# Delta stage: 32x32 blocks turned on VectorE and placed by transfers, in place of transposes on TensorE

## The chip, the core and the metric

The kernel runs on one core of one Trainium2 chip. The metric is the device time of one execution in microseconds (us). The core has TensorE (PE in the profile, with PEld for its weight loads), VectorE (DVE), ScalarE (ACT), GpSimd (POOL), and SyncE (SP), which here issues nearly all transfers (DMAs), in order.

## What is computed

A row of 1024 tokens of width 256 passes four blocks with residual additions: an attention block, a first mixture of experts, a gated delta rule layer, and a second mixture of experts. The change lies in the gated delta rule layer (`_L1_attn_ref`), 32 value heads on 16 key heads, chunks of 64 tokens, cut here to its core:

```python
qkv = silu(causal_conv1d(qkv, conv_weight))            # per channel, 4 taps
q, k = l2norm(q) * Dk ** (-0.5), l2norm(k)
attn = -(k_beta @ k.T * decay_mask), strictly lower    # per chunk
attn = (I - attn)^-1                                   # row by row in the reference
value_corrected = attn @ v_beta
k_cumdecay = attn @ (k_beta * exp(g))
for c in chunks:                                       # carries the state
    v_prime = value_corrected - k_cumdecay @ state
    out = q @ state * exp(g) + (q @ k.T * decay) @ v_prime
    state = state * exp(g_last) + (k * kd).T @ v_prime
core = rmsnorm(out * silu(z), norm_weight)
x = x + core @ W_out
```

## The kernel before

All work of the layer is in `delta1_phase`. It takes the key heads one after another; what belongs to one key head (one key, one query, GR = 2 value heads) is called a round here, g = 0 to 15. Tokens lie in TT = 8 tiles of 128. The code handles the state in steps t = 0 to 7 of 128 tokens.

Of one round, these are the steps, under the names in the order tables. On TensorE `proj j c` projects key, query and two values (j = 0 to 3) with channels on the partitions, `products i` multiplies keys by keys and queries, and `kturn`, `qturn`, `vturn h` transpose eight 128x128 tiles each, so that tokens lie on the partitions. `l0p, l0y, l0x, l1p, l1y, l2p, l2y` build the inverse of a 128x128 matrix out of its solved 16x16 diagonal blocks, in many small matmuls. `gates i` project z. `ks, qs, y, kv, iv` with a step number carry the state: ks and y make the corrected values, kv the new state, qs and iv the output. `out_turn b` transposes eight tiles of the normalised output and `out_mm b i` multiplies them by W_out, for halves b = 0, 1. VectorE has the convolution taps (`tap`, line 1647), the scaling of keys, values and outputs (`kb`, `vturn` 1711, `yn` 1786), the product with the decay (`products` 1702), the residual `r` 1757, the state 1766, the sum `gather` 1779 and the addition to x (1792). ScalarE has the first tap and silu, the decay's exp, the squares for the norms (`ksq`, `qsq`, `sq2`), and copies out of PSUM (`kturn` 1823, `ys` 1911, `out_turn` 1926). GpSimd solves the 16x16 blocks (`solve`), scales keys (`kout` 1952), applies the gate (`gate` 1988) and the norm's power (`norm`).

SyncE moves, per round, the 16x16 blocks out to DRAM and back in another layout (`blocks`, lines 1355 and 1359), the solved blocks out and back (`solved`, 1377 to 1384), decay rows (`rows`), weights of the round after next (`weights` 1320) and a slice of W_out (`wo` 1348). So the inverse of a round hangs on this chain: products of VectorE (semaphore `ai_s`), `blocks`, `solve`, `solved`, `l0p`.

The order of the work is written out by hand, one table for each engine (`PE_ORDER`, `DVE_ORDER`, `ACT_ORDER`, `POOL_ORDER`, `SP_ORDER`), run once for each round. In the table `this` stands for the round's own state part, `next` for the projections and products of the round after it, and `prev` for what is left of the round before. `loop` writes the steps in that order, so each engine has a fixed sequence, and its waits are on semaphores.

## Time and profile before

| | us |
|---|---|
| median of 3 runs | 2077.16 (2075.91 to 2077.48) |
| the profiled execution, its own time | 2069.65 |
| its span on the core | 2067.9 |
| first matmul of the delta layer to the last addition to x | 622.00 to 1844.3 |
| start of l0p in round 1, 14 and 15 | 764.54, 1704.47, 1774.98 |
| PE, DVE, ACT, POOL busy over the span | 1650.5, 1178.3, 894.6, 569.4 |

The page gives busy time of each engine and its costliest lines. It lists a median time to landing only for some transfers. The timeline gives instructions in order of time, merged where they follow each other: start, duration, engine, line, operation, output from input, count, and in brackets the idle time before it with what ended it. "issue" is idle time in which the engine waited for nothing that the profile shows. Matmuls are pipelined, so the distance from one start to the next says more than a duration. A matmul in 32 bits is two records; a transpose is one.

### The profile page before, as it was taken

What the parts mean: (1) busy time and instruction counts of PE and PEld (TensorE: products, weight loads), DVE (VectorE), ACT (ScalarE), POOL (GpSimd) and SP (SyncE); (2) the same over time, 40 slices, a digit from 0 to 9 for tenths busy, and PEclk for the clock granted to TensorE, in tenths of its full rate; (3) what the DMA queues carried; (4) which work ended last, traced back from release to release, by engine and by line L of the source; (5) the groups of instructions that cost most, each with busy time, mean ns of one, the idle gap of its engine ahead of it and who ended that gap; (6) DMA issues with size and microseconds to landing.
All of it is one profiled execution on the core that took longest, in us unless ns stands there. A gap on an engine that the chain in (4) does not pass through costs nothing. (4 is left out here: it accounts for less than half of the span.)

```text
span 2067.9 us, 43100 instructions
## 1 busy us (share of the span) xinstructions
PE 1650.5 (80%) x16669; PEld 1199.2 (58%) x16669; DVE 1178.3 (57%) x2439; ACT 894.6 (43%) x2414; POOL 569.4 (28%) x958
## 2 busy tenths in 40 slices
PE   5878952566025899999999999999999999857998
PEld 2443341455012677777777767777777777744555
DVE  6774149111545467667667666776676677333444
ACT  2225920112014464655665566566556556321111
...
GB/s 208 1 2 2 1 70 1 124 155 130 166 20 50 39 46 27 26 51 35 22 48 51 27 26 52 38 37 30 51 33 23 50 35 12 16 1 31 38 38 43
DMA packets 175331, 95.95 MB, mean 46 GB/s; under 512 B 98467, under 2 KB 165923, under 8 KB 175136
## 3 DMA queue, kind: packets, MB, share of 16 engines
...
## 5 line engine op out<-in xcount | busy, mean ns | idle before, releaser
L1647 DVE SCALAR_TENSOR_TENSOR d_conv<-d_big,d_cw,d_conv 128x1023 f32<-128x1023 f32 (+2 forms) x192 | 245.3, 1278 | 42.9 <-ACT d_conv L1808 40.0
L1406 PE MATMUL d_big<-all_xn_t,d_w 128*128 128x512 f32 x512 | 248.3, 614 | 26.4 <-DMA d_w<-in_L_attn_W_qkvz 15.5
L1988 POOL TENSOR_TENSOR d_y<-d_y,all_xn 128x256 f32<-128x256 f32 x128 | 96.5, 754 | 259.3 <-DVE d_y L1779 217.8
L1406 PEld LDWEIGHTS d_big<-all_xn_t,d_w 128*128 128x128 f32 x512 | 95.7, 197 | 105.9 <-issue 90.5
L1619 PE MATMUL d_big<-d_wo,d_yt 128*128 128x256 f32 x512 | 145.7, 442 | 3.7 <-issue 2.8
L1944 POOL TENSOR_TENSOR d_sv<-d_ek,d_half 128x8 f32<-128x8 f32 x16 | 26.2, 1637 | 425.7 <-DVE d_ek L1673 396.3
L2150 PE MATMUL e_gu<-all_xn_t,e_up_w 128*128 128x512 f32 x272 | 121.9, 602 | 15.4 <-DMA e_dn_w<-in_L_ffn_Wd 15.4
L1808 ACT ACTIVATE d_conv<-d_big,d_cw 128x1024 f32<-128x1024 f32 x64 | 71.4, 1116 | 134.0 <-issue 78.3
L1619 PEld LDWEIGHTS d_big<-d_wo,d_yt 128*128 128x128 f32 x512 | 111.8, 227 | 22.9 <-issue 4.1
L1911 ACT COPY d_ys<-d_big 128x128 f32<-128x128 f32 x256 | 60.4, 268 | 142.9 <-PE d_big L1575 123.8
L1549 PE MATMUL d_big<-d_w,all_xn_t 128*128 128x256 f32 x512 | 118.3, 379 | 1.5 <-DVE d_vs L1711 1.5
L1549 PEld LDWEIGHTS d_big<-d_w,all_xn_t 128*128 128x128 f32 x512 | 96.0, 190 | 27.1 <-issue 14.4
L1702 DVE SCALAR_TENSOR_TENSOR d_AI<-d_big,d_b_col,d_decay 128x256 f32<-128x256 f32 x256 | 105.8, 476 | 6.6 <-PE d_big L1436 6.6
L323 DVE TENSOR_REDUCE a_neg_max<-a_big 128x1 f32<-128x128 f32 (+7 forms) x128 | 90.0, 752 | 32.7 <-PE a_big L256 32.6
L1918 ACT ACTIVATE d_junk<-d_y 128x128 f32<-128x128 f32 x256 | 79.8, 312 | 47.3 <-POOL d_y L1988 43.0
L2150 PEld LDWEIGHTS e_gu<-all_xn_t,e_up_w 128*128 128x128 f32 x272 | 52.5, 193 | 74.6 <-issue 73.8
L147 PE MATMUL ln_turned<-all_ident,all_xn 128*128 128x128 f32 x64 | 17.5, 443 | 91.0 <-DVE all_xn L127 91.0
L473 ACT ACTIVATE a_probs<-a_big 128x512 f32<-128x512 f32 (+3 forms) x192 | 77.0, 513 | 20.6 <-PE a_big L406 18.5
L1973 POOL TENSOR_TENSOR d_blk_ty<-d_blk_ty,d_blk_p 128x15 f32<-128x15 f32 (+7 forms) x240 | 80.2, 334 | 18.8
L2183 DVE TENSOR_TENSOR e_h<-e_act_g,e_gu 128x512 f32<-128x512 f32 x34 | 23.4, 687 | 107.3 <-ACT e_act_g L2171 107.3
L1786 DVE TENSOR_TENSOR d_y<-d_y,d_rn 128x1024 f32<-128x1024 f32 x32 | 43.4, 1357 | 68.0 <-POOL d_rn L2004 68.0
L2171 ACT ACTIVATE e_act_g<-e_gu 128x512 f32<-128x512 f32 x34 | 20.3, 597 | 142.4 <-PE e_gu L2150 142.4
...
## 6 DMA issues: line engine op xcount, KB each, us to landing
...
c_rows<-ranked_scratch SPq DMA_DIRECT2D x4, 1024.0 KB
c_rows<-ranked_scratch ACTq DMA_DIRECT2D x4, 1024.0 KB
...
```

The source lines that it names most:

```text
L323: dve.tensor_reduce(neg_max[:, h, q:q + 1], big[2 + q % 2][:, :, :].rearrange("p c n -> p (c n)")[:, 0:(q + 1) * P], AX.X, ALU.max, negate ...
L473: act.activation(probs[:, n % NPB, off:512], bank[n % NST][:, off:512], ACT.Exp).then_inc(exp_done, 1)
L1406: mm = pe.matmul(big[0][:, c, :], w_sb[par][:, k, n * DK:(n + 1) * DK], xn_t[:, k, c * 512:(c + 1) * 512], start=(k == 0), stop=(k == KD - 1))
L1549: mm = pe.matmul(bank[6 + i % 2][:, (t % 2) * 256:(t % 2) * 256 + 256], xn_t[:, k, t * P:(t + 1) * P], w_sb[par][:, k, 4 * DK:6 * DK], sta ...
L1619: mm = pe.matmul(bank[6 + i][:, r * 256:r * 256 + 256], yt[:, h, 2 * i + r, :], wo_sb[:, h, :], start=(h == 0), stop=(h == GR - 1), skip_g ...
L1647: dve.scalar_tensor_tensor(conv[:, sh:T], src[:, 0:T - sh], cw[:, bass.ds(g, 1), COLUMN_OF[j], 3 - sh], conv[:, sh:T], ALU.mult, ALU.add). ...
L1702: ins = dve.scalar_tensor_tensor(AI[par][:, h * TT + t, :, :], bank[6 + i % 2][:, (t % 2) * 256:(t % 2) * 256 + 256].rearrange("p (a i) -> ...
L1808: act.activation(conv[:, :], big[0][:, :, :].rearrange("p c n -> p (c n)"), ACT.Copy, scale=cw[:, bass.ds(g, 1), COLUMN_OF[j], 3]).then_in ...
L1918: act.activation(junk[:, :], y[:, t, h, :], ACT.Square, accum_out=ss2[:, i:i + 1]).then_inc(s["sq2_s"], 1)
L1973: pool.tensor_tensor(T_[:, j + 1:BL, 0:j + 1], T_[:, j + 1:BL, 0:j + 1], blk_p[:, 0:rows, 0:j + 1], ALU.subtract).then_inc(s["sol_v"], 1)
L1988: pool.tensor_tensor(part, part, zs[:, t, :], ALU.mult).then_inc(s["yg_s"], 1)
L2150: mm = pe.matmul(gu_ps[c][:, n, :], up_w[par][:, n, k, :], xn_t[:, k, c * 512:(c + 1) * 512], start=(k == 0), stop=(k == KD - 1))
```

## The change

- `kturn`, `qturn`, `vturn`, `out_turn` leave TensorE and ScalarE. In their place VectorE turns each 32x32 block within its own 32 partitions (`kq_turn a`, `v_turn h`, `y_turn b`, all STREAM_TRANSPOSE of 128x1024), and SyncE places the blocks by way of DRAM: `kq_out a`, `kq_in a`, `v_out`, `v_in`, `y_out b`, `y_in b`.
- The values are scaled in place by GpSimd (`vs`), which also takes over `yn` and `cross` from VectorE. norm_weight is multiplied into W_out once a round (`wo` on GpSimd).
- The squares of q are taken from SBUF. `products 0` waits for silu and the gates' buffers only.
- All five order tables are new. `out_mm 0` moves from its own round into the next, `proj 2` and `proj 3` stand elsewhere, and steps 2 to 5 of the state follow each other with little between.

```diff
 SP_ORDER
-    this rows, solved, weights; next blocks; prev wo
+    this solved, v_in; next kq_out 0, kq_in 0; prev y_out 0; next kq_out 1; this weights; next kq_in 1, rows; prev y_in
+    0, y_out 1; next blocks; prev y_in 1, wo; next v_out
...
+            def kq_out(g, par, a):
+                sp.wait_ge(s["kq_x"], g * 2 + a + 1)
...
+                sp.dma_start(kq_dram[a].rearrange("q r b n -> (q r) b n"),
+                             turned[:, :, a * TT:(a + 1) * TT, :].rearrange("p b t r -> p b (t r)")).then_inc(s[f"kq_out{a}"], 16)
+            def kq_in(g, par, a):
...
+                    if a == 0:
+                        sp.wait_ge(s["kout_s"], g * 2)
...
+                sp.wait_ge(s[f"kq_out{a}"], g * 16 + 16)
+                for b in range(NQ):
+                    sp.dma_start(kq_tok[QB * b:QB * b + QB, :, a * TT:(a + 1) * TT, :].rearrange("p q t r -> p q (t r)"),
+                                 kq_dram[a, :, :, b, :].rearrange("q r n -> r q n")).then_inc(s[f"kq_in{a}"], 16)
+            def v_out(g, par):
+                sp.wait_ge(s["v_x"], g * 2 + 2)
...
+                sp.dma_start(v_dram.rearrange("q r b n -> (q r) (b n)"), turned[:, :, :, :].rearrange("p b a r -> p (b a r)")
+                             ).then_inc(s["v_out"], 16)
+            def y_in(g, par, b):
...
+                sp.wait_ge(s["y_out"], g * 128 + 64 * b + 64)
+                for q in range(NQ):
+                    sp.dma_start(yt[:, :, QB * q:QB * q + QB], y_dram[q].rearrange("e r (a n) -> (e r) a n", n=QB)
+                                 ).then_inc(s["yt_in"], 16)
...
 on TensorE
-            def kturn(g, par):
-            def qturn(g, par):
-            def vturn(g, par, h):
-            def out_turn(g, par, b):
...
 on VectorE
-            def vturn(g, par, h):
-            def yn(g, par, b):
+            def v_turn(g, par, h):
+                dve.wait_ge(s["silu_s"], g * NJ + h + 3)
...
+                dve.transpose(turned[:, :, h * TT:(h + 1) * TT, :], vt[:, :].rearrange("p (t q r) -> p q t r", q=NQ, r=QB)
+                              ).then_inc(s["v_x"], 1)
...
 on ScalarE
-            def kturn(g, par):
-            def out_turn(g, par, b):
...
 on GpSimd
+            def vs_(g, par, h):
...
+                pool.tensor_tensor(mine, mine, sv[:, :].unsqueeze(1).unsqueeze(3).broadcast_to([P, NQ, TT, QB]), ALU.mult
+                                   ).then_inc(s["vs_s"], 1)
+            def yn(g, par, b):
```

TensorE around l0p of one round. Before (in the names, d_X and d_Y are the solved blocks, all_ident marks a transpose, d_w the projections and gates, d_wo out_mm):

```order
L1549 MATMUL d_big<-d_w,all_xn_t 128x256 x4
L1406 MATMUL d_big<-all_xn_t,d_w 128x512 x2
L1463 MATMUL d_big<-d_X,d_AI 32x16 x64
L1610 MATMUL d_big<-all_ident,d_y 128x128 x8
L1474 MATMUL d_big<-d_Y,d_P 32x32 x64
L1486 MATMUL d_big<-d_P,d_Y 32x32 x48
L1619 MATMUL d_big<-d_wo,d_yt 128x256 x8
L1499 MATMUL d_big<-d_Xc,d_AI 32x32 x32
L1414 MATMUL d_big<-all_ident,d_kq 128x128 x8
L1406 MATMUL d_big<-all_xn_t,d_w 128x512 x2
```

And with the change:

```order
L1610 MATMUL d_big<-d_S,d_kq 128x256
L1623 MATMUL d_big<-d_rv,d_Y 128x128 x2
L1475 MATMUL d_big<-all_xn_t,d_w 128x512 x4
L1505 MATMUL d_big<-d_X,d_AI 32x16 x64
L1641 MATMUL d_big<-d_ys,d_AI 128x128 x2
L1516 MATMUL d_big<-d_Y,d_P 32x32 x64
L1528 MATMUL d_big<-d_P,d_Y 32x32 x48
L1475 MATMUL d_big<-all_xn_t,d_w 128x512 x4
L1541 MATMUL d_big<-d_Xc,d_AI 32x32 x32
L1594 MATMUL d_big<-d_w,all_xn_t 128x256 x4
```

The transposes between l0p and l0y and behind l1p are gone. Behind l0x stands the projection of the next round's j = 2 where out_mm stood, and behind l1p a gates step.

SyncE between the blocks of one round and the solved blocks that l0p needs. Before:

```order
L1355 DMA blocks_scratch<-d_AI 16x16x16 x8
L1359 DMA d_blk_at<-blocks_scratch 128x256
L1348 DMA d_wo<-in_L_attn_W_out 128x2x256
L1328 DMA d_G<-decay_rows_scratch 64x4x256
```

And with the change, in that place and up to the first load of solved blocks:

```order
L1363 DMA blocks_scratch<-d_AI 16x16x16 x8
L1367 DMA d_blk_at<-blocks_scratch 128x256
L1453 DMA d_yt<-turned_y_scratch 128x8x32 x4
L1356 DMA d_wo<-in_L_attn_W_out 128x2x256
L1423 DMA turned_v_scratch<-d_turned 128x2048
L1385 DMA solved_scratch<-d_blk_ty 128x512
L1391 DMA d_X<-solved_scratch 16x16x16
```

The decay rows are gone from ahead of the solved blocks (they stand earlier now), and the 1024 KB of turned values go out directly ahead of them.

## Rows read from the trace of the kernel before

**Rows 1.** Windows: stretch, length, busy PE, PEld, DVE, ACT, POOL, granted clock, DMA share, GB/s.
```profile
772.00:776.00 4.00, 3.40 (x85) 3.07 (x86) 1.60 (x3) 3.07 (x4) 0.00 (x0) 0.50 0.02 4
...
1260.00:1330.00 70.00, 67.31 (x880) 53.29 (x879) 50.43 (x92) 43.30 (x124) 29.21 (x56) 1.00 0.18 39
```

**Rows 2.** Timeline of TensorE, the start of l0p in rounds 0, 1, 8, 9, 15.
```profile
693.79 1.91 PE L1463 MATMUL d_big<-d_X,d_AI 32*32 32x16 f32 x128 [4.79 <-DMA d_Y<-solved_scratch]
...
764.54 1.26 PE L1463 MATMUL d_big<-d_X,d_AI 32*32 32x16 f32 x128
...
1275.62 1.25 PE L1463 MATMUL d_big<-d_X,d_AI 32*32 32x16 f32 x128
...
1343.89 1.26 PE L1463 MATMUL d_big<-d_X,d_AI 32*32 32x16 f32 x128
...
1774.98 1.90 PE L1463 MATMUL d_big<-d_X,d_AI 32*32 32x16 f32 x128 [2.84 <-DMA d_Y<-solved_scratch]
```

**Rows 3.** Timeline of TensorE, a set of eight transposes and the step behind it.
```profile
1218.08 1.09 PE L1414 MATMUL d_big<-all_ident,d_kq 128*128 128x128 f32 x8
1219.01 1.88 PE L1406 MATMUL d_big<-all_xn_t,d_w 128*128 128x512 f32 x4
```

**Rows 4.** Timeline of TensorE, idle in the small matmuls of rounds 5 and 15.
```profile
1063.56 0.71 PE L1474 MATMUL d_big<-d_Y,d_P 32*32 32x32 f32 x59 [1.18 <-issue]
...
1066.91 0.50 PE L1486 MATMUL d_big<-d_P,d_Y 32*32 32x32 f32 x27 [1.88 <-issue]
...
1783.20 0.25 PE L1486 MATMUL d_big<-d_P,d_Y 32*32 32x32 f32 x4 [1.19 <-issue]
```

**Rows 5.** Timeline of TensorE, steps of the state: ks 5, then kv 5.
```profile
1249.07 0.68 PE L1558 MATMUL d_big<-d_S,d_kq 128*128 128x128 f32 x4
...
1251.05 0.71 PE L1584 MATMUL d_big<-d_ys,d_kout 128*128 128x128 f32 x4 [0.24 <-ACT d_ys L1911]
```

**Rows 6.** Timeline of TensorE ahead of l0p of round 8: vturn 1 and gates 3.
```profile
1258.94 1.06 PE L1414 MATMUL d_big<-all_ident,d_vt 128*128 128x128 f32 x8
...
1271.95 1.89 PE L1549 MATMUL d_big<-d_w,all_xn_t 128*128 128x256 f32 x8
```

**Rows 7.** Groups by line: busy us, mean ns of one, then idle before and what ended it.
```profile
L1647 DVE SCALAR_TENSOR_TENSOR d_conv<-d_big,d_cw,d_conv 128x1023 f32<-128x1023 f32 (+2 forms) x192 | 245.3, 1278 | 42.9 <-ACT d_conv L1808 40.0
...
L1786 DVE TENSOR_TENSOR d_y<-d_y,d_rn 128x1024 f32<-128x1024 f32 x32 | 43.4, 1357 | 68.0 <-POOL d_rn L2004 68.0
...
L1952 POOL TENSOR_TENSOR d_kout<-d_k_tok,d_kxb 128x1024 f32<-128x1024 f32 x32 | 61.5, 1921 | 2.6 <-POOL d_blk_ty L1978 0.2
...
L1711 DVE TENSOR_TENSOR d_vs<-d_big,d_sv 128x1024 f32<-128x1024 f32 x32 | 38.9, 1216 | 4.6 <-PE d_big L1414 4.5
...
L1816 ACT ACTIVATE d_vt<-d_conv 128x1024 f32<-128x1024 f32 x32 | 33.9, 1061 | 5.7 <-DVE d_conv L1647 5.2
```

**Rows 8.** Timeline of SyncE's queue: first load of round 0, then blocks and solved of round 8.
```profile
686.49 0.33 SPq L1383 DMA_DIRECT2D d_X<-solved_scratch  x1
...
1243.52 3.74 SPq L1355 DMA_DIRECT2D blocks_scratch<-d_AI  x8
...
1265.19 0.33 SPq L1377 DMA_DIRECT2D solved_scratch<-d_blk_ty  x1
1267.22 0.33 SPq L1383 DMA_DIRECT2D d_X<-solved_scratch  x1
```

**Rows 9.** Two transfers of 1024 KB: DMA issues (us to landing), timeline of SyncE's queue.
```profile
tokens_scratch<-all_xn SPq DMA_DIRECT2D x1, 1024.0 KB, 5.9
...
2062.68 0.38 SPq L2204 DMA_DIRECT2D out<-all_x  x1
```

**Rows 10.** Windows, while the solved blocks (3072 pieces of 64 bytes) are loaded.
```profile
1267.20:1275.60 8.40, 8.36 (x33) 5.59 (x32) 4.01 (x4) 5.26 (x19) 6.88 (x7) 1.00 0.31 32
```

**Rows 11.** Timeline of the last round: VectorE's yn 1, then TensorE's out_mm.
```profile
1832.88 1.22 DVE L1786 TENSOR_TENSOR d_y<-d_y,d_rn 128x1024 f32<-128x1024 f32 x1 [4.16 <-POOL d_rn L2004]
...
1837.00 6.57 PE L1619 MATMUL d_big<-d_wo,d_yt 128*128 128x256 f32 x16 [0.87 <-ACT d_yt L1926]
```

More of the change, by code:

```diff
@@ new lines @@
+    0, proj 1 1; this l0p; prev iv 7; this l0y, l0x; next proj 2 0, proj 2 1; this l1p, gates 3, l1y; next products 0;
+    this l2p 0, l2p 1; next proj 3 0; this l2y 0; next products 1; this l2y 1; next products 2; this y 0; next products
+    3; this kv 0; next proj 3 1; this ks 1, iv 0, qs 1, y 1; prev out_mm 0 0; this kv 1, iv 1, ks 2; prev out_mm 0 1;
+    this y 2, qs 2, kv 2, iv 2, ks 3, qs 3, y 3, kv 3, iv 3, ks 4, qs 4, y 4, kv 4, iv 4, ks 5, qs 5, y 5, kv 5, iv 5;
+    prev out_mm 1 0; this ks 6; prev out_mm 1 1; this y 6, qs 6, kv 6
@@ L1188 @@
 """)
 DVE_ORDER = steps_of("""
-    prev state 6, r 7, gather 6; this vturn 1; next shift 0, tap 0 1, tap 0 2, tap 0 3, shift 1; prev gather 7, yn 1;
-    this l0p; next tap 1 1, tap 1 2; this qe; next tap 1 3; this l0x; prev out_mm 1 0, out_mm 1 1; next cross; this l1p,
-    l1y, l2p; next tap 2 1; this l2y; next tap 2 2, kb; this state 0, gather 0, r 1; next tap 2 3, products 0; this
-    state 1; next products 1; this r 2; next products 2; this state 2, gather 1, r 3; next products 3; this gather 2,
@@ L1195 @@
-    gather 3, state 3, r 4; next vturn 0; this state 4, gather 4, r 5, yn 0, state 5; next tap 3 1; this r 6; next tap 3
-    2, tap 3 3; this gather 5, out_mm 0 0, out_mm 0 1
+    next shift 0, tap 0 1, tap 0 2; prev r 7; next tap 0 3; prev gather 6; next shift 1; this qe; next kq_turn 0; prev
+    y_turn 0; next tap 1 1; this l0p; next tap 1 2; prev gather 7; next tap 1 3; this l0x; next kq_turn 1; this l1p;
+    next tap 2 1, tap 2 2; this l1y; next tap 2 3; this l2p; next kb, products 0; this l2y; next products 1, products 2;
@@ L1197 @@
+    this state 0; prev y_turn 1; this r 1; next products 3; this gather 0, state 1, gather 1, r 2; prev out_mm 0 0; next
+    tap 3 1; this state 2, r 3, gather 2, state 3, r 4, gather 3, state 4, r 5, gather 4; prev out_mm 0 1; this state 5;
+    next v_turn 0, tap 3 2; this r 6; next tap 3 3; this gather 5; prev out_mm 1 0; this state 6; next v_turn 1; prev
+    out_mm 1 1
 """)
 ACT_ORDER = steps_of("""
-    next tap0 0; prev o1 7; this gates 0, gates 1; prev ys 7, sq2 5, sq2 6, sq2 7; this gates 2; next silu 0; this gates
@@ L1201 @@
[L1201 to L1204 removed]
+    prev sq2 2; next tap0 0; prev o1 6; this gates 0; prev sq2 3; this gates 1; prev sq2 4; next silu 0; prev o1 7, ys
@@ L1205 @@
+    7; next tap0 1; prev sq2 5; next decay; this gates 2, l0y; next silu 1; prev sq2 6; next tap0 2; this l1p; next ksq
+    0, ksq 1, ksq 2, ksq 3; this l1y, gates 3, l2p; prev sq2 7; this l2y, ys 0; next qsq 0; this o1 1, ys 1; next silu
+    2, tap0 3; this ys 2, o1 2, ys 3, o1 3, ys 4, o1 4, ys 5, sq2 0, o1 5; next qsq 1; this ys 6; next silu 3; this sq2
+    1
 """)
 POOL_ORDER = steps_of("""
-    this solve 2, solve 3, solve 4; prev gate 5; this kout; prev gate 6, gate 7, norm 1; next kb; this gate 0, gate 1,
@@ L1391, in _ @@
             sp.wait_ge(s["const_s"], 12)
-            loop(sp, SP_ORDER, dict(blocks=blocks, solved=solved, weights=weights_after, rows=rows_after, wo=wo_after))
+            loop(sp, SP_ORDER, dict(kq_out=kq_out, kq_in=kq_in, v_out=v_out, v_in=v_in, y_out=y_out, y_in=y_in, blocks=blocks, solved=solved, weights=weights_after, rows=rows_after, wo=wo_after))
         @block.tensor
```

247 lines of the change are left out of this document (140 added, 107 removed).

## The prediction

> **What bounds the kernel now.** First the windows over the delta stage, in stretches of 70 us: TensorE is busy 65 to 67 us of 70, VectorE 50, ScalarE 43, GpSimd 29, and the transfer engines 18% [rows 1]. So a round costs what TensorE's list costs, plus what TensorE waits. Second the timeline of TensorE by round, at the start of l0p: from round 1 to 15 it is (1774.98 - 764.54) / 14 = 72.2 us a round, and the leanest, round 8, takes 1343.89 - 1275.62 = 68.3 us [rows 2]. Third, what the 3.9 us between the two are: inside l0y and l0x TensorE stops twice with no releaser ("issue"), 1.18 and 1.88 us in round 5 [rows 4], and behind such a pair, in round 1, the granted clock is 0.50 from 772 to 776, its lower level of 1.2 GHz, where it is 1.00 through the lean round [rows 1]. Fourth, SyncE's queue: from the end of products (`ai_s`, 1243.52) to l0p (1275.62) 32.1 us pass [rows 2, 8], and l0p starts directly as the last solved blocks land. So the chain of the inverse has no slack today; TensorE's list and that chain are in balance.
>
> **What leaves TensorE.** Eight transposes take 1219.01 - 1218.08 = 0.93 us [rows 3]; a round has six such sets (kturn, qturn, two vturn, two out_turn): 6 x 0.93 = 5.6 us. All lies on the path, since TensorE is the bound: 72.2 - 5.6 = 66.6. The Trainium skill (VectorE: DVE Perf Modes, Rules for kernel authors) speaks against the change: transpose 128x128 on TensorE if PSUM will do. By that rule, as I read it, the saving would be nothing or less. The row shows what it is worth here, 0.12 us for a tile on the engine that is the bound.
>
> **What VectorE gets.** It loses two vturn of 1.22 us, two yn of 1.36 [rows 7] and cross (about 1.2, the same length of row): 6.4 us. It gets six STREAM_TRANSPOSE of 128x1024. The trace has none. The nearest row is the scaling of the same 1024 elements, 1.22 us; the other end is twice that, 2.4, and nothing suggests less than 1.2. I take 1.25, so 7.5 us against 6.4, and VectorE stays at some 48 of 68 us. At 2.4 it would be 55, still no bound, but one of the six lies on a path, below.
>
> **GpSimd** gets two scalings of values, two yn, cross and the W_out product. By kout, 1.92 us for 1024 elements [rows 7], that is 5 x 1.92 + 1 = 10.6 us: 29 becomes some 40 of 68. Not the bound. ScalarE loses one copy and four halves of a copy, 3 to 4 us.
>
> **State steps in a row.** Steps 2 to 5 have no filler now. From ks 5 to kv 5 is 1.98 us for three steps that need 1.35 [rows 5], and the same again at kv to ks; such a step costs about 0.7 us more than its matmuls. Before, the two steps that stood alone and the short waits round y 0, y 1 and step 2 summed to about 3 us; with the new table I count 2.6. I put this at nothing. Two small waits are new: l2p has only products 0 (0.9 us) ahead of it to cover VectorE's copy, which stands behind a tap of 1.28 us [rows 7]: 0.6 us. And VectorE has tap 1 1 ahead of l0p's result, which costs up to 1.1 us in a round where TensorE does not wait at l0p, and nothing where it does.
>
> **The wait that the change adds.** SyncE sends v_out (1024 KB) directly ahead of `solved`, whose result l0p needs. v_out waits for v_turn 1, which waits for silu 3, behind ys 6 on ScalarE. Both sides start at kv 6. On TensorE, the steps between kv 6 and l0p are those of before without vturn and with iv 6 and gates 3 changed: 1275.62 - 1258.94 = 16.7, less 0.9, less gates 3 at 1.8 [rows 2, 6] = 14.0 us. On the other side: from the end of kv 6 silu 3 and v_turn 1 end 2.0 us later (1.06 + 1.25, begun just before kv 6 starts [rows 7]); v_out lands 5.9 us after its issue by the other store of 1024 KB, or at most 5.2 by the last store of the kernel, issued at 2062.68 in a span that ends at 2067.9 [rows 9]; the 256 KB of `solved` alone take 2.0 us (1265.19 to 1267.22), of which I let 1.0 stand behind v_out (0 to 2.0); from there to l0p it is 7.3 us in round 0 (686.49 to 693.79) and 8.4 in round 8 [rows 2, 8]. Sum 15.5 to 17.3, or 1.5 to 3.3 us more than TensorE's 14.0; I take 2.4. Queued behind v_out on SyncE are `solved`, v_in and kq_out 0, kq_in 0; who waits is l0p, and TensorE idles.
>
> A wait before l0p gives something back: in round 15, which waits 2.84 us there [rows 2], only one issue gap of 1.19 us follows instead of two of 3.1 in sum [rows 4]. I take 1.0 us. So a round is 66.6 + 0.6 + 2.4 - 1.0 = 68.6; without that wait it would be 66.6 + 0.6 + 1.1 = 68.3. The two agree, which makes 68.5 likely: 72.2 - 68.5 = 3.7 us saved, over 15 rounds 56 us.
>
> **Other transfers.** I count from the start of l0p, by the list of steps; an issue on SyncE takes 3.74 / 8 = 0.47 us [rows 8]. k: v_in's four issues end at about 0.5, kq_out 0 is behind them and lands, with v_in's 1024 KB ahead of it, at 5 to 6. kout on GpSimd, which kq_in 0 waits for too, ends at about 4, eight steps behind solve. Then four issues and a landing of 2 us: 9 to 10. Squares on ScalarE for 3.5 us make 13, and products 0 on VectorE has to be done by 20, when products 2 wants its buffer on TensorE, so the landing is needed by some 13. y: y_in 0 is issued behind the weights (which wait for gates 3, at 12), kq_in 1 and the decay rows, at 17 to 19, and lands at 23; out_mm 0 0 comes at 27. y_in 1 is issued behind blocks, at 34, and lands at 40; out_mm 1 0 comes at 42, behind iv 5. The blocks leave at 28 instead of 36 after l0p, which gives the chain of the inverse (32.1 us from there) its slack: 28 + 32 = 60, were it not for v_out. All hidden, with 2 to 4 us of cover; if one is gone, TensorE stops by what is missing, once a round. Bytes: 6 MB a round more on a queue that is busy 18% [rows 1].
>
> **Prologue and epilogue.** The prologue gains and loses about the same: k and q take 4 to 6 us longer to reach their squares, but products no longer waits for the squares of q. The epilogue is exposed. Before, from the end of yn (1832.88 + 1.22) to out_mm (1837.00) 2.9 us pass [rows 11]. Now each half takes y_turn 1.25, four issues of 0.47 and a landing of 2 for y_out, the same four issues and some 5.4 for y_in: 12.4 us. The two halves overlap in part, but y_in 1 waits until out_mm 0 has read its tile. I get 12 us more at the end (7 to 20).
>
> **Sum.** Against the profiled execution's 2069.65: - 56 + 12 = - 44, 2026. The three runs have a median of 2077.16, 7.5 above that execution; the same difference against it is 2033.
>
> **Rivals.**
> A, the forecast: a round of 67.5 to 69.7 us, 2018 to 2051. For it: two ways of counting meet there.
> B, the tables fit closer than I count, nothing new waits: 66.6 us, 15 x 5.6 = 84 less, 12 more: 2005. For it: v_out's data may go in parallel with `solved`, and tap 1 1 may be early enough. Against it: both go down one queue, in order.
> C, slower: the same place, l0p behind v_out. If block transposes take 2.4 us (1.2 more), v_out 5.9, `solved` its full 2.0 behind it and the loads 8.4, the wait is 2.0 + 1.2 + 5.9 + 2.0 + 8.4 - 14.0 = 5.5 us, and if nothing is given back at the issue gaps, a round takes 66.6 + 0.6 + 5.5 = 72.7. That is 8 us more in 15 rounds, and the epilogue: 2097. It decides from a round of 71.4, a wait of 4.2 us. For it: TensorE lost its clock behind the 2.84 us of round 15, where l0p took 1.90 us instead of 1.26 [rows 2]. Against: it takes all high ends.
> D, slower: the pieces of 128 bytes of y_in (4096 for each half). In the loads of solved blocks 31% of 16 engines over 8.4 us moved 3072 pieces of 64 bytes [rows 10], 14 ns a piece. At that price a half takes 3.6 us. The other end is the store in pieces of 1 KB, 5.9 us for 1024 of them [rows 9], 92 ns with all latency in it. From about 39 ns on, y_in 1 makes out_mm 1 0 and ks 6 wait 3 us a round; at 45 ns both halves wait, some 8 us in sum, and 15 x (68.5 + 8 - 72.2) + 12 gives 2154. The Trainium skill (DMA: Bandwidth & Descriptors, Specifications) asks for 512 bytes or more for line rate; it would make such pieces dear. The solved blocks show that pieces of 64 bytes are not.
> The change does what it says, by the order of instructions; that it would not is no case.
>
> **How the numbers follow.** A 0.42, B 0.17, C 0.20, D 0.07, and 0.14 for a round between 69.7 and 71.8 (some cover gone once), which is 2051 to 2083 and holds most of "same". Time: that of A. Range: from B's 2000 up to 2098, which takes C in and leaves D out. Within 0.2% (4 us, about what this kernel's measurement can tell) I put 0.06; faster 0.42 + 0.17 + 0.08 = 0.67; slower 0.27.
>
> **What would show it.** TensorE's transposes gone and l0p to l0p at 68 to 69 us in the middle rounds. Before l0p an idle time of 1.5 to 3.3 us that ends with a DMA of the solved blocks: right for A. If none, B. If over 4, C. The landing of v_out and of `solved` in the list of DMA issues. STREAM_TRANSPOSE at 1.2 or 2.4 us. out_mm waiting on d_yt by a DMA says D. products on VectorE waiting for kb would say that the k path was longer than I placed it. The stretch from yn 1 of the last round to the last addition to x, 12 us longer. I would be wrong most easily if a wait that I call covered, by 2 to 4 us, is not.

## The result, and the profile after

The changed kernel takes 2056.5 us (median of 4 runs, 2055.2 to 2060.0), the kernel before 2076.5 on the same chip (2073.2 to 2077.5). The ratio is 0.9908, 95% interval 0.9891 to 0.9925. On a second chip it was 0.9933 (0.9911 to 0.9954). So it is faster, by 20 us where 44 were forecast. The profiled execution took 2057.01 us with a span of 2055.3, which is 12.6 less than the profiled execution before.

The timeline of TensorE at the start of l0p (L1505 now) in rounds 1, 8, 14 and 15. In brackets is the idle time before the row, with what ended it.

```profile
763.54 1.25 PE L1505 MATMUL d_big<-d_X,d_AI 32*32 32x16 f32 x128 [1.30 <-DMA d_Y<-solved_scratch]
...
1255.84 1.26 PE L1505 MATMUL d_big<-d_X,d_AI 32*32 32x16 f32 x128
...
1672.86 1.26 PE L1505 MATMUL d_big<-d_X,d_AI 32*32 32x16 f32 x128
...
1742.65 1.90 PE L1505 MATMUL d_big<-d_X,d_AI 32*32 32x16 f32 x128 [6.85 <-DMA d_Y<-solved_scratch]
```

A round is (1672.86 - 763.54) / 13 = 69.95 us, where it was (1704.47 - 764.54) / 13 = 72.30. That is 2.35 saved, not 3.7. The windows over these 13 rounds, before and after (the columns are those of [rows 1]):

```profile
764.54:1704.47 939.93, 880.98 (x11312) 698.93 (x11311) 639.10 (x1144) 563.21 (x1612) 345.95 (x638) 0.97 0.17 37
```

```profile
763.54:1672.86 909.32, 822.10 (x10687) 632.62 (x10687) 684.60 (x1157) 522.57 (x1546) 486.60 (x718) 0.93 0.56 129
```

TensorE is busy 58.9 us less, 4.5 a round instead of the 5.6 of six sets of transposes, since its granted clock fell from 0.97 to 0.93. It is idle 909.32 - 822.10 = 87.2 us instead of 59.0, 2.2 a round more. 72.3 - 4.5 + 2.2 is the 69.95. The waits of TensorE in that stretch say where (us in total, times, longest). First before, then after:

```profile
PE d_big L1486 <- issue: 19.5, 10, 2.2
PE d_big L1474 <- issue: 17.6, 12, 1.8
```

```profile
PE d_big L1516 <- issue: 44.8, 13, 5.2
PE d_big L1516 <- DVE d_P L1770: 10.0, 10, 1.3
PE d_big L1528 <- issue: 9.1, 6, 1.8
PE d_big L1505 <- DMA d_Y<-solved_scratch: 7.6, 8, 2.2
PE d_big L1661 <- DMA d_yt<-turned_y_scratch: 5.5, 5, 1.5
PE d_big L1641 <- issue: 5.5, 1, 5.5
```

L1474 and L1486 were l0y and l0x, now L1516 and L1528. L1641 is iv 7, which now stands between l0p and l0y. Idle time there that no semaphore explains grew from 37.1 to 59.4 us, from 2.9 to 4.6 a round. This is the larger part of what is missing.

**What "issue" is here.** The timeline of TensorE in round 7:

```profile
1187.45 1.25 PE L1505 MATMUL d_big<-d_X,d_AI 32*32 32x16 f32 x128 [0.95 <-DMA d_Y<-solved_scratch]
1188.70 0.68 PE L1641 MATMUL d_big<-d_ys,d_AI 128*128 128x128 f32 x4
1189.66 1.13 PE L1516 MATMUL d_big<-d_Y,d_P 32*32 32x32 f32 x111 [0.27 <-DVE d_P L1770]
1194.68 0.47 PE L1516 MATMUL d_big<-d_Y,d_P 32*32 32x32 f32 x17 [3.89 <-issue]
1194.92 1.90 PE L1528 MATMUL d_big<-d_P,d_Y 32*32 32x32 f32 x96
1196.75 4.86 PE L1475 MATMUL d_big<-all_xn_t,d_w 128*128 128x512 f32 x8
```

TensorE stops in the middle of l0y, at 1190.8. The list of DMA queues has a queue of kind "instruction". In the quarter of a microsecond from 1191.75 it begins one packet of 0.02 MB (packets, MB, share of 16 engines):

```profile
q1 hardware_dynamic: 39, 0.05, 98.0%
q8 instruction: 1, 0.02, 33.0%
```

That share of 0.25 us is 1.32 us of one engine. The packet starts at about 1192.0, and the gap ends at 1194.68. Before, ahead of the 1.18 us gap of round 5 [rows 4], the same view of the quarter from 1061.00:

```profile
q1 hardware_dynamic: 23, 0.04, 44.4%
q8 instruction: 1, 0.02, 23.3%
```

That packet took 0.93 us and began at about 1061.2, 1.2 us before TensorE ran dry at 1062.38. The later one began 1.2 us after TensorE ran dry. From l0p of round 1 to l0p of round 14 the kernel before has 23 idle times of 1 us or more on TensorE, and all 23 end 1.1 to 1.7 us behind the end of such a packet. Their packet starts on average 0.65 us before the idle time does. After the change 30 idle times are that long. 11 of them end with a semaphore. The 19 marked issue all end 1.2 to 1.6 us behind the end of a packet, which starts on average 0.53 us after the idle time does.

What is late is the start of the packet and not its length: over these 13 rounds a packet takes 1.08 us in the mean before and 1.13 after. But the first one behind the start of l0p begins 2.1 us after it before, and 4.8 us after it with the change.

So what is missing are TensorE's instructions, which come by DMA. In this run of small matmuls they are used up faster than they come. The Trainium skill (Runtime: NRT & Kernel Launch, Instruction fetch mechanics) says that an engine's sequencer fetches its instructions in blocks of 16 KiB by a DMA queue of its own. The packets of 0.02 MB agree. It calls the cost mostly hidden, and here the trace doesn't agree: 59.4 us of idle in 13 rounds. What filled the engines meanwhile is seen in the windows of the same stretch:

```profile
1189.00:1192.00 3.00, 1.51 (x115) 1.24 (x113) 3.00 (x5) 2.94 (x4) 2.17 (x2) 1.00 1.09 242
1192.00:1195.00 3.00, 0.32 (x23) 0.32 (x26) 0.23 (x1) 1.73 (x2) 1.49 (x1) 0.55 0.55 178
```

The DMA share is 1.09 at 242 GB/s: v_in and kq_out 0, issued at 1186.1 and 1188.2. In the kernel before, the same place of round 5 reads:

```profile
1061.00:1064.00 3.00, 1.82 (x127) 1.56 (x127) 2.96 (x4) 2.94 (x4) 0.00 (x0) 1.00 0.07 25
```

There the share is 0.07. From 1.5 to 4.5 us after the start of l0p the share is 0.23 in the mean of the 13 rounds before, and 1.05 after. What in the engines holds the packet back these views don't show; that the bulk transfers do it is tried below. After the change the granted clock also falls from 1.00 to the lower level of 1.2 GHz while TensorE waits, and the projection behind it (L1475) runs slow, 4.86 us for eight matmuls that take 3.60 at the full clock (1252.31 to 1255.84).

The order of SyncE around l0p of round 8:

```profile
1209.22 9.47 SPq L1453 DMA_DIRECT2D d_yt<-turned_y_scratch  x4
...
1243.83 0.34 SPq L1423 DMA_DIRECT2D turned_v_scratch<-d_turned  x1
1244.37 0.32 SPq L1385 DMA_DIRECT2D solved_scratch<-d_blk_ty  x1
1248.39 0.32 SPq L1391 DMA_DIRECT2D d_X<-solved_scratch  x1
```

Groups by line, the new operations of VectorE and GpSimd (busy us, mean ns of one, idle before):

```profile
L1756 DVE STREAM_TRANSPOSE d_turned<-d_vt 128x1024 f32<-128x1024 f32 x32 | 39.7, 1242 | 1.5 <-ACT d_vt L1870 1.4
L2066 POOL TENSOR_TENSOR d_y<-d_y,d_rn 128x1024 f32<-128x1024 f32 x32 | 60.7, 1897 | 2.5
```

### The profile page after: what moved, and what is told of

It reads as the page before. It is cut to its first block and busy times, and to the rows that moved or that the text cites. A ratio compares the mean times of both kernels' runs of the same rounds, so it can differ in the third digit from the quotient of the medians.

```text
span 2055.3 us, 42263 instructions
## 1 busy us (share of the span) xinstructions
PE 1579.2 (77%) x15901; PEld 1117.7 (54%) x15901; DVE 1225.2 (60%) x2456; ACT 845.9 (41%) x2334; POOL 742.0 (36%) x1053
## 5 line engine op out<-in xcount | busy, mean ns | idle before, releaser
L1475 PE MATMUL d_big<-all_xn_t,d_w 128*128 128x512 f32 x512 | 274.1, 675 | 37.5 <-DVE d_conv L1690 22.0
L2044 POOL TENSOR_TENSOR d_y<-d_y,all_xn 128x256 f32<-128x256 f32 x128 | 115.7, 904 | 230.9 <-DVE d_y L1837 123.7
L1475 PEld LDWEIGHTS d_big<-all_xn_t,d_w 128*128 128x128 f32 x512 | 103.4, 218 | 141.6 <-issue 121.1
L1661 PE MATMUL d_big<-d_wo,d_yt 128*128 128x256 f32 x512 | 126.2, 392 | 24.4 <-DMA d_yt<-turned_y_scratch 23.6
L1661 PEld LDWEIGHTS d_big<-d_wo,d_yt 128*128 128x128 f32 x512 | 95.7, 197 | 37.3 <-issue 19.2
L1822 DVE SCALAR_TENSOR_TENSOR d_S<-d_S,l_gamma,d_big 128x128 f32<-128x128 f32 x192 | 58.4, 345 | 69.6 <-PE d_big L1632 69.4
L1949 ACT ACTIVATE d_o<-d_big,l_cols 128x128 f32<-128x128 f32 x224 | 70.0, 365 | 46.0 <-issue 35.5
L1641 PE MATMUL d_big<-d_ys,d_AI 128*128 128x128 f32 x512 | 81.7, 283 | 6.9 <-issue 5.5
L1780 DVE COPY d_Xc<-d_big 32x512 f32<-32x512 f32 x48 | 32.8, 684 | 89.0 <-PE d_big L1528 88.0
L2054 POOL TENSOR_TENSOR d_rn<-d_ss,d_inv_width 128x8 f32<-128x8 f32 x32 | 7.4, 233 | 212.3 <-ACT d_junk L1965 212.1
```

Source lines behind the costliest of these rows:

```text
L1475: mm = pe.matmul(big[0][:, c, :], w_sb[par][:, k, n * DK:(n + 1) * DK], xn_t[:, k, c * 512:(c + 1) * 512], start=(k == 0), stop=(k == KD - 1))
L1641: mm = pe.matmul(bank[5][:, h * DK:(h + 1) * DK], AI[par][:, h * TT + t, 1, :], ys[:, h, :], start=True, stop=True, skip_group_check=True)
L1661: mm = pe.matmul(bank[6 + i][:, r * 256:r * 256 + 256], yt[:, (2 * i + r) * GR + h, :], wo_sb[:, h, :], start=(h == 0), stop=(h == GR - 1) ...
L1949: act.activation(o1[:, t % 2, h, :], bank[4][:, h * DK:(h + 1) * DK], ACT.Copy, scale=col(C_IN, t, h, g)).then_inc(s["o1_s"], 1)
L2044: pool.tensor_tensor(part, part, zs[:, t, :], ALU.mult).then_inc(s["yg_s"], 1)
```

## Experiments

Two theories stood against each other first. **Bulk**: the megabytes of v_in and kq_out 0 stand directly behind the solved blocks, flow just while TensorE has its small matmuls, and make its instruction blocks late. **Cover**: out_turn 1 lay between l0p and l0y, and its 0.93 us hid the fetch, so taking it away gave nothing, whatever the transfers do.

Every run was timed beside the kernel before on its chip. Chips differ by some 30 us ahead of the delta layer, so totals are compared as difference to the kernel before on the same chip. The kernel as changed stands at -20.0 in the result and at -13.4 in e13. A round is from l0p of round 1 to l0p of round 14, divided by 13. Issue idle is that of l0y and l0x, and of iv 7 or the transposes where they stand between, per round.

| run | us | to before | ratio (interval) | round | issue idle | clock |
|---|---|---|---|---|---|---|
| before | 2076.5 | | | 72.30 | 2.9 | 0.97 |
| changed | 2056.5 | -20.0 | 0.9908 (0.9891 to 0.9925) | 69.95 | 4.6 | 0.93 |
| e1 few bytes, v and k | 2013.9 | -56.8 | 0.9722 (0.9693 to 0.975) | 66.99 | 1.7 | 0.95 |
| e2 before + bulk | 2125.3 | +54.7 | 1.0255 (1.0226 to 1.0284) | 75.82 | 5.4 | 0.94 |
| e3 proj 2 0 inside | 2067.0 | -3.7 | 0.998 (0.9959 to 1.0001) | 71.17 | 4.0 | 0.93 |
| e4 v_in late | 2034.4 | -36.3 | 0.9816 (0.9786 to 0.9846) | 68.76 | 1.8 | 0.94 |
| e5 before + bulk, ahead of wo | 2181.4 | +112.4 | 1.0531 (1.05 to 1.0563) | 81.02 | 3.2 | 0.92 |
| e6 and y_in 0 early | 2032.2 | -36.7 | 0.9815 (0.979 to 0.9841) | 68.62 | 2.2 | 0.93 |
| e7 and VectorE's l0p first | 2038.3 | -30.7 | 0.9846 (0.9811 to 0.9882) | 68.90 | 2.8 | 0.94 |
| e8 last y on TensorE | 2048.5 | -20.4 | 0.9898 (0.9876 to 0.9919) | 70.62 | 4.9 | 0.92 |
| e9 before + bulk, behind wo | 2047.2 | +4.4 | 1.0028 (1.0013 to 1.0043) | 72.30 | 2.9 | 0.97 |
| e10 e6 and e8 | 1997.4 | -45.5 | 0.9781 (0.9758 to 0.9804) | 68.06 | 2.2 | 0.95 |
| e11 eight transposes more | 2039.9 | -2.9 | 0.9994 (0.9981 to 1.0007) | 71.06 | 5.0 | 0.94 |
| e12 e1 and few bytes in v_out | 1978.8 | -64.1 | 0.9691 (0.967 to 0.9712) | 66.34 | 1.0 | 0.95 |
| e13 changed, again | 2028.7 | -13.4 | 0.9933 (0.9911 to 0.9954) | 70.14 | 4.7 | 0.93 |
| e14 few bytes, v_in alone | 1985.5 | -56.6 | 0.9731 (0.9713 to 0.9749) | 67.22 | 2.1 | 0.95 |
| e15 few bytes, k alone | 2028.6 | -13.5 | 0.9942 (0.9923 to 0.9961) | 70.04 | 4.4 | 0.92 |
| e16 eight transposes, again | 2039.8 | -2.2 | 0.9987 (0.9972 to 1.0002) | 70.99 | 5.1 | 0.94 |

### e1: few bytes in v_in, kq_out 0 and kq_in 0

```diff
-                sp.dma_start(vs[par][...].rearrange("p q a r -> p q (a r)"), v_dram[:, :, b, :]...
+                sp.dma_start(vs[par][...].rearrange("p q a r -> p q (a r)")[:, :, 0:16], v_dram[:, :, b, 0:16]...
```

> The changed kernel, but v_in, kq_out 0 and kq_in 0 move 16 of 512 (or 256) values of each piece: the same number of issues, waits and pieces, a thirty-second (sixteenth) of the bytes. The values and the keys are therefore wrong. Theory 1 (bulk): TensorE's idle time in l0y and l0x is the time of its own instruction blocks (16 KB packets on queue 8), which arrive late because the 1.5 MB of these transfers fill the transfer engines in just those 6 us. Then the idle time marked issue in l0y and l0x falls from 4.6 us a round to about 3 (single gaps of 1.2 to 2.2 instead of up to 5.2), time at the lower clock falls from 9.7 us a round towards 5, and the kernel takes about 15 x 3 = 45 us less, 2010 (2000 to 2025), unless the solved blocks then set the pace at l0p. Theory 2 (cover): the gaps have grown since out_turn 1 no longer lies between l0p and l0y, whatever the transfers do. Then gaps and clock stay, and the time stays within 6 us of 2056.

Measured: 36.8 us less than the changed kernel by the difference to before (43.4 if e13 is taken for it), and issue idle of 1.7 us a round. Bulk holds and cover falls. A round is now 66.99 us, which is the 72.2 - 5.6 of the forecast and little more.

### e2: the kernel before with bulk transfers behind the solved blocks

```diff
-    this rows, solved, weights; next blocks; prev wo
+    this rows, solved, bulk, weights; next blocks; prev wo
+            def bulk(g, par):
...
+                for b in range(4):
+                    sp.dma_start(more[32 * b:32 * b + 32, :]..., more_dram[:, :, b, :]...).then_inc(s["more_in"], 16)
+                sp.dma_start(some_dram, xn_t[:, 0, :]).then_inc(s["some_out"], 16)
```

> The kernel before, with transfers added that nothing waits for but themselves: behind the solved blocks, once a round, four loads of 256 KB like v_in and one store of 512 KB like kq_out. Theory 1 (bulk): idle time marked issue in l0y and l0x grows from 3.1 us a round to 4.5 or more, single gaps to 3 to 5 us, the time at the lower clock from 4.7 us a round to some 8, and the kernel takes 30 to 50 us more than 2076. Theory 2 (cover): no change, within 6 us of 2076, since the order on TensorE is that of before; the weights, which stand behind, are not needed for tens of us.

Measured: 54.7 us more, a little above the 30 to 50 expected, with nothing changed on any compute engine but one fill of the added tile at the start. TensorE's waits:

```profile
PE d_big L1491 <- issue: 52.2, 13, 5.5
PE d_big L1503 <- issue: 16.1, 10, 2.6
```

All 25 idle times of 1 us or more again end 1.2 to 1.6 us behind the end of an instruction packet, which now starts 0.44 us after the idle time does. The first packet behind the start of l0p begins 4.6 us after it, where it is 2.1 without the transfers. The transfers alone make what the change made, in a kernel that still has out_turn 1 ahead of l0y.

### e3: proj 2 0 between l0y and l0x

```diff
-    this l0y, l0x; next proj 2 0, proj 2 1; this l1p
+    this l0y; next proj 2 0; this l0x; next proj 2 1; this l1p
```

> The changed kernel with proj 2 0 between l0y and l0x instead of behind l0x: four matmuls of 512 columns, some 0.9 us of work that asks for few instructions. If the small matmuls outrun the supply of instructions in any case, 0.9 us of other work in their midst hides up to 0.9 us of the gap inside l0x, 0.5 to 0.9 us a round, so 8 to 14 us less than 2056. Against it: l0x ends later by 0.9 us and so does l1p, if proj 2 1 alone doesn't cover VectorE's copy, which is 0.68 us: then nothing or up to 5 us more.

Measured: 71.17 us a round, 1.2 more than the changed kernel. Issue idle as counted in the table falls by 0.6 a round: l0x then has none, where it had 9.1 us in sum. But 3.9 us of it come back in l1p (L1541), which had none, so 0.3 a round is won. The gap in l0y, ahead of the filler, is as it was (46.0 us). The wait for y_in 0 grows from 5.5 to 17.1 us. Why y_in 0 comes later there was not followed up. A miss: the filler stood behind the longer gap, not in it.

### e4: v_in behind kq_in 0

```diff
-    this solved, v_in; next kq_out 0, kq_in 0; prev y_out 0
+    this solved; next kq_out 0, kq_in 0; this v_in; prev y_out 0
```

> The changed kernel with v_in behind kq_in 0 in SyncE's queue instead of directly behind the solved blocks; its 1 MB then flows 8 us later, behind l0x. Theory 1 (bulk): the first instruction block behind l0p comes on time, the second too, gaps of 1.2 to 2.2 us as before the change, 1.5 us a round less idle and some 2 us with the clock: 2020 to 2040. Theory 2 (cover): gaps unchanged, 2050 to 2062. Risk for both: kq_out 0 goes earlier, vs 0 on GpSimd gets its values later, and y 0 would wait for them.

Measured: 16 us less than the changed kernel, as the first theory said. The first packet behind the start of l0p is back at 2.1 us after it. Issue idle falls below that of the kernel before, but y_in 0, which now stands behind v_in, comes late:

```profile
PE d_big L1661 <- DMA d_yt<-turned_y_scratch: 17.1, 10, 4.1
...
PE d_big L1528 <- issue: 12.6, 6, 2.5
...
PE d_big L1516 <- issue: 8.6, 9, 2.0
```

### e5 and e9: the same bulk transfers in the kernel before, elsewhere in the queue

```diff
-    this rows, solved, weights; next blocks; prev wo
+    this rows, solved, weights; next blocks; this bulk; prev wo
```

> The kernel before with the same added transfers as in the run before (1.5 MB a round that nobody needs), but issued behind blocks, some 30 us before l0p, while TensorE has the state steps and large matmuls. Theory 1 (bulk): it is the place that costs, since there TensorE uses up its instructions slowly: within 8 us of 2072, where the same transfers directly behind the solved blocks gave 2125; idle marked issue in l0y and l0x stays at 3 us a round. Rival (amount): 1.5 MB more a round cost the same wherever they stand, by pressure on all other transfers (blocks, solved, weights): 2105 to 2130.

Measured: +112.4 us, a miss by the total. The waits tell why, and that the first theory isn't touched: issue idle is 3.2 us a round as before, and W_out comes 5.75 us late each round.

```profile
PE d_big L1636 <- DMA d_wo<-in_L_attn_W_out: 74.7, 13, 6.9
PE d_big L1491 <- issue: 22.3, 12, 2.4
PE d_big L1503 <- issue: 19.1, 10, 2.4
```

So the same was put behind wo:

```diff
+    this rows, solved, weights; next blocks; prev wo; this bulk
```

> The kernel before with the added 1.5 MB a round behind wo instead of ahead of it, since ahead of it they held up W_out by 5.75 us a round, and that, not TensorE's instructions, gave 2181. (They are left out in the last round.) Theory 1 (bulk): idle marked issue in l0y and l0x stays at 3.1 us a round, and the time is within 10 us of 2072, unless the decay rows, which stand behind now, come late. Rival (amount): 2105 or more with issue idle of 4.5 us or more.

```profile
PE d_big L1493 <- issue: 20.3, 12, 2.2
PE d_big L1505 <- issue: 17.8, 10, 2.2
```

Measured: +4.4 us, issue idle 2.9 a round, the round 72.30 as before. The same 1.5 MB a round cost 55 us in one place of SyncE's queue, 4 in another and 112 in a third. So the amount by itself costs no more than these 4 us (ratio 1.0013 to 1.0043, and in that run the last round does without them); the rest is the place.

### e6 and e7: y_in 0 early, and VectorE's result of l0p ahead of the tap

```diff
+    this solved; next kq_out 0, kq_in 0; prev y_out 0; this v_in; prev y_in 0; next kq_out 1; this weights; next kq_in 1, rows; prev y_out 1
```

> The changed kernel with v_in behind y_out 0 and y_in 0 directly behind v_in, ahead of kq_out 1, weights, kq_in 1 and rows. Against the run with v_in moved alone (2034): out_mm 0 0 there waited 17 us in 10 rounds for y_in 0. If that wait is the place in the queue, it goes, and the time is 2034 - 17 = 2017 (2012 to 2028). If it is the price of 4096 pieces of 128 bytes, it stays or moves to products, which then wait for k, and the time stays at 2030 to 2040.

Measured: the wait for y_in 0 is gone, and the time is that of e4 all the same (-36.7 against -36.3). In its place TensorE waits 6.7 us at products for the squares of k, and the issue idle of l0y is 14.3 us instead of 8.6. So it was the place in the queue that made out_mm wait, but moving it gave nothing: it is given back in two other waits. The expectation had the time of 2012 to 2028 for the place alone, and 2030 to 2040 with a wait of products for k for the price of the pieces. The time is the second one. How much of that wait is due to the 4096 pieces of 128 bytes that now stand ahead of k, and how much to any transfer in that place, no run separates.

```diff
-    next tap 1 1; this l0p; next tap 1 2
+    this l0p; next tap 1 1, tap 1 2
```

> The run before with VectorE's result of l0p ahead of tap 1 1 instead of behind it. l0y waited for that result 10 us in 13 rounds, by the prediction's 1.1 us a round where TensorE doesn't wait at l0p. If these waits lie on the path: 5 to 10 us less than the run before it. If the time comes back as a longer instruction gap in l0y (the block is fetched in parallel to that wait): within 3 us of it.

Measured: no gain, -30.7 with an interval that touches e6's. The wait of l0y for VectorE is gone, and the issue idle in the same l0y is longer by most of it. Two rows of e6, then the one of e7:

```profile
PE d_big L1516 <- issue: 14.3, 11, 2.5
...
PE d_big L1516 <- DVE d_P L1770: 9.6, 11, 1.3
```

```profile
PE d_big L1516 <- issue: 21.8, 13, 2.5
```

That fits a block that is fetched beside that wait. In the mean of 13 rounds l0y starts 0.66 us earlier after the start of l0p than in e6 (2.29 against 2.95) and ends 0.20 us earlier (5.60 against 5.80). So while a block is missing anyway, most of a wait ahead of l0y is free. l0x still ends 0.47 us earlier (8.03 against 8.50). The gain is lost behind it, where the rest of the round takes 60.86 us instead of 60.12, 0.2 of that in the wait of products for the squares (9.0 us in sum against 6.7).

### e8 and e10: the last round's y on TensorE

```diff
+                    if at(g, HK - 1):
...
+                        for e in range(GR * 4):
+                            mm = pe.transpose(bank[e // 4][:, (e % 4) * P:(e % 4 + 1) * P], y[:, 4 * b + e // GR, e % GR, :], ident[:, :])
```

> The changed kernel, but in the last round alone y goes the old way: eight transposes on TensorE and a copy out of PSUM by VectorE for each half, no y_turn, y_out, y_in. In the changed kernel from the end of yn 1 to the last addition to x it takes 21.0 us, in the kernel before 10.2. If that is the way through DRAM: 10 to 11 us less than 2056, so 2046, and the stretch falls to some 10. The rest of the 20 us by which the end behind the last l0p is longer, 9 us, is ahead of yn 1: if it is TensorE's lower clock behind the long wait at l0p of round 15, as I think, it stays here.

The last yn on GpSimd and the last addition to x on VectorE, first as changed, then e8:

```profile
1809.14 1.90 POOL L2066 TENSOR_TENSOR d_y<-d_y,d_rn 128x1024 f32<-128x1024 f32 x1
...
1831.36 0.69 DVE L1842 TENSOR_TENSOR all_x<-all_x,d_big 128x512 f32<-128x512 f32 x1 [2.13 <-PE d_big L1661]
```

```profile
1823.04 1.90 POOL L2089 TENSOR_TENSOR d_y<-d_y,d_rn 128x1024 f32<-128x1024 f32 x1
...
1832.11 0.69 DVE L1865 TENSOR_TENSOR all_x<-all_x,d_big 128x512 f32<-128x512 f32 x1 [1.04 <-PE d_big L1678]
```

From the end of yn to the end of the addition it takes 7.9 us instead of 21.0. But yn itself comes 4 us later behind l0p of round 15, since VectorE's gather 7 now stands behind the copy of the first half. The end behind that l0p is 9.0 us shorter (89.4 to 80.4). The total doesn't resolve it (-20.4 against -20.0 and -13.4), as the rounds of this run were 0.67 us longer. Put into e6 it does:

> The changed kernel with v_in late, y_in 0 early (2032) and the last round's y on TensorE (8 us less): if both are independent, 2024 (2018 to 2028).

Measured: -45.5 against e6's -36.7, so 9 us less, as the stretch says. This is the fastest version that computes everything: 0.9781 of the kernel before, and 0.985 of the changed kernel by the quotient of e10 and e13 (1997.4 and 2028.7, both on chips where the kernel before takes 2042 to 2043).

### e11 and e16: eight transposes put back ahead of l0y

```diff
             def l0y(g, par):
+                for t in range(8):
+                    pe.transpose(bank[3][:, (t % 4) * P:(t % 4 + 1) * P], ident[:, :], ident[:, :])
                 pe.wait_ge(s["p0_s"], g + 1)
```

> The changed kernel with eight transposes of the identity more between iv 7 and l0y, where out_turn 1 stood in the kernel before; their result isn't used. 16 x 0.93 = 15 us more work on TensorE. Theory 1: l0y's gap ends when the instruction block is there, whatever TensorE does meanwhile, so they are hidden in the gap, which shrinks by up to 0.9 us from 3.4 a round: 2056 to 2062, so taking out_turn 1 away there gave nothing. If the block is only asked for once the instructions ahead of it are used up, the gap moves with them: 2069 to 2074.

> The changed kernel with eight transposes more ahead of l0y, beside the kernel as changed on one chip. In the first such run the gaps in l0y and l0x were as long as without them (4.3 us a round), so I now expect that nothing hides them: 12 to 17 us more. If the gap covers them: 0 to 5 us more.

Measured: on one chip 2039.8 against 2028.7 for the kernel as changed, 11.2 us more (rounds 70.99 against 70.14). Of the 0.93 us of work 0.85 shows. TensorE's wait for VectorE takes in some (10.9 to 2.1 us in sum), the issue idle takes in none: it is 5.1 us a round instead of 4.7. My expectation for e11 was wrong, that for e16 right but for 1 us. So cover falls for good: the transposes don't move the fetch (the first packet begins 4.7 us after the start of l0p, in e13 4.9), and taking out_turn 1 away there gave nearly what it took. Where the 0.85 us arise can be followed from the start of l0p, in the mean of 13 rounds: l0y ends 0.27 us later than in e13 (8.96 against 8.69), l0x 0.58 later (11.82 against 11.24), and the rest comes behind. So by the end of l0y most of the 0.93 is absorbed here too, as in e7, by the wait for VectorE; the loss is made behind it, in l0x above all, whose issue idle is 13.9 us instead of 9.7. Why l0x loses it again stays open.

### e13, e14, e15: which transfer

> The changed kernel as it is, as the measure for the three runs beside it on the same chip. A ratio of 0.991 to before, as in the result, and a round of 69.5 to 70.5 us.

> The changed kernel with few bytes in v_in alone (values wrong, keys right). Moving v_in behind kq_in 0 gave 20 us. If v_in's megabyte, directly behind the solved blocks, is the main cause, few bytes give most of the 43 us of both: 28 to 40 us less than the kernel as changed, and idle marked issue in l0y and l0x falls from 4.1 us a round to some 2. If it is just the megabyte's time ahead of kq_out 0, half or less: 10 to 20.

> The changed kernel with few bytes in kq_out 0 and kq_in 0 alone (keys wrong, values right). By the first theory a small part: 3 to 15 us less than the kernel as changed, issue idle stays above 3 us a round, since v_in still fills the engines while l0y's blocks are fetched. By the second 20 or more.

Measured: e14 takes 43.2 us less than e13 on the same chip (28 to 40 expected), e15 0.1. In e14 the first packet begins 2.0 us after the start of l0p, in e15 4.7, in e13 4.9. All of e1's gain is v_in's. First e14, then e15:

```profile
PE d_big L1516 <- issue: 14.2, 12, 2.7
PE d_big L1528 <- issue: 11.8, 6, 2.4
```

```profile
PE d_big L1518 <- issue: 42.8, 13, 4.3
```

e15 was expected at 3 to 15 and gave nothing. Of e14's 2.92 us a round, 2.5 are idle time and 0.4 are busy time at a better clock (0.95 instead of 0.93). e4 and e6 moved v_in and took the issue idle down as far, but a round there is still 1.4 us longer than e14's: the megabyte is in someone's way wherever it flows.

### e12: few bytes in v_out too

> As the run with few bytes in v_in and k (2014), and v_out too moves 16 of 512 values of each piece (values and keys wrong). If v_out's megabyte is what delays the solved blocks, their landing falls from 4.0 us to 2.0 and l0p's wait of 0.54 us a round goes: up to 7 us less, 2007 to 2014. By the prediction's term for this wait, 2.4 us a round, it would be 30 us less, since TensorE's list would then set the pace.

```profile
PE d_big L1507 <- DMA d_Y<-solved_scratch: 1.1, 1, 1.1
```

Measured: l0p's wait for the solved blocks falls from 7.0 us in e1 to 1.1, a round from 66.99 to 66.34, the difference to before from -56.8 to -64.1. So v_out does delay the solved blocks, as the prediction said, for 0.5 us a round and not for 2.4.

## Why the prediction was half right

Faster was forecast and came, but with 20 us instead of 44.

**Right.** The bound, and what transposes are worth on it: without v_in's bytes a round is 67.2, where 66.6 was the sum without any wait. So the rule of the Trainium skill that spoke against the change (VectorE: DVE Perf Modes, Rules for kernel authors) doesn't decide it where TensorE is the bound: v_in's bytes, not the transposes on VectorE, took the gain. STREAM_TRANSPOSE takes 1.24 us (1.25 taken). GpSimd's yn takes 1.90 (1.92), and GpSimd did not become the bound. TensorE's side from kv 6 to l0p: 1242.1 to 1255.84 is 13.7 us (14.0). y_in 0's cover of 4 us was thin: out_mm 0 0 waited in 5 of 13 rounds, 0.4 us a round, and in round 7 its four issues alone took 9.47 us on SyncE. The k path stayed hidden. D was far off: in the last round 2108 pieces of 128 bytes went in 2 us,

```profile
q1 hardware_dynamic: 2108, 0.27, 84.7%
```

which is 0.847 x 16 x 2000 / 2108 = 12.9 ns of one engine for a piece, where D began at 39.

**Wrong: "I take 1.0 us", what a wait before l0p gives back at the issue gaps.** This is the step that failed. I read from round 15 [rows 2, 4] that a wait ahead makes the gaps in l0y and l0x shorter. That was weak already in the kernel before: round 8 has a single gap there, of 1.21 us, without any wait at l0p. And round 15 had no transfers beside it, its DMA share was 0.02. With the change v_in flows just there, and the gaps grew by 1.7 us a round instead. The wait did next to nothing: the 8 rounds that waited at l0p had 4.5 us of issue idle each, the 5 that did not 4.7, and round 15, behind its 6.85 us, has gaps of 3.19 in l0y and 2.27 ahead of l1p. The clock took 1.1 us more out of the 5.6 of the transposes; that it is the gaps that lower it is likely by the windows above, and was not tried by itself. The prediction gave v_in a place in the queue, ahead of k, and never asked who else uses the transfer engines at that time. "Bytes: 6 MB a round more on a queue that is busy 18%" was the average over a round; in the 3 us that mattered, the share was 1.09 in round 7. e2, e9 and e14 show it, and e14 its size: 2.9 us a round and 43 us in all.

**Mis-sized: the wait of l0p behind v_out, 2.4 us.** It is 7.6 / 13 = 0.58. From the issue of v_out to the landing of `solved` it takes 1248.39 - 1243.83 = 4.6 us, where I had 5.2 to 5.9 for v_out and 1.0 on top. The packets of the two follow each other: the last of v_out's 128 (8 KB each) ends at 1247.35, the first of `solved` begins at 1247.20. So the 1.0 on top was right, and v_out's time was too long: 3.5 us from its issue to the end of its data (3.7 in the mean of 13 rounds). The 5.9 came from a store in pieces of 1 KB [rows 9], and v_out's pieces are 8 KB; that the size of the pieces makes the difference was not tried.

**Mis-sized: the state steps in a row, "nothing".** TensorE's waits for ys, r and the state (6.1, 5.2 and 2.8 us in 13 rounds) are gone from the list, 1.1 us a round won. Tap 1 1 ahead of l0p's result cost 10.0 / 13 = 0.8 where I had up to 1.1, but by e7 most of that time the fetch would have stood there anyway.

**How they add up.** The forecast of 68.6 with what was measured: + 2.7 for the issue gaps (1.7 more instead of 1.0 less), + 1.1 for the clock, - 1.8 for the wait at l0p, - 1.1 for the state steps, - 0.6 for a wait of l2p that is not in the list, + 0.8 for tap 1 1, + 0.4 for y_in 0. That is 70.1, where 69.95 was measured. So the round came out only 1.4 above the forecast because other terms erred the other way. That was luck: with the failed step and the clock alone it would be 72.4, no gain.

**Mis-sized: the end, 12 us.** From l0p of round 15 to the last addition it takes 1832.05 - 1742.65 = 89.4 us instead of 69.3, 20.1 more. The way of y through DRAM is 21.0 - 10.2 = 10.8 of it. Between iv 7 and the end of yn 1 are 3.9 more, since gate and yn on GpSimd follow each other (10.4 instead of 6.5). The last 5.4 lie between l0p and iv 7. The windows of that stretch, in this order before, after, and in e2 (the kernel before with the bulk transfers):

```profile
1774.98:1827.55 52.57, 46.32 (x754) 40.30 (x755) 21.91 (x50) 19.13 (x64) 7.32 (x11) 0.84 0.02 7
```

```profile
1742.65:1800.62 57.97, 49.26 (x750) 43.72 (x750) 20.01 (x49) 19.00 (x69) 15.94 (x18) 0.71 0.28 60
```

```profile
1826.63:1885.11 58.48, 49.17 (x754) 42.40 (x754) 21.90 (x50) 19.16 (x64) 7.06 (x11) 0.77 0.12 32
```

And e14, with few bytes in v_in:

```profile
1672.09:1725.70 53.61, 47.38 (x751) 41.95 (x751) 20.02 (x49) 19.01 (x69) 15.47 (x17) 0.76 0.23 46
```

The clock is 0.71 instead of 0.84, behind a wait of 6.85 us at l0p instead of 2.84. The wait is not the main cause. e14 waits 7.99 us there, and its stretch takes 53.61 us, 1.0 more than before. e2 waits 3.20 us, and its stretch takes 58.48, 5.9 more. In e13 it is 56.78 behind a wait of 7.90. So v_in's bytes are the larger part here too: issue idle in the stretch is 1.2 us before, 5.5 after, 4.3 in e2 and 3.0 in e14.

**The ledger.** Start of l0p in round 0: +2.6. From there to l0p of round 15: -34.9. Behind it +20.1, and -0.3 in the last phases: -12.6, the difference of the two profiled executions. The medians differ by 20.0; the execution of the kernel before that was profiled lies 7 us under its median.

**Open.** After e14 the clock is still 0.95 where it was 0.97 before, with less idle time (51.9 us of marked waits against 56.7). Why it falls earlier behind l0p now isn't settled.
